# Mixture of 14 experts: GpSimd's indirect transfers in bursts of four, each burst gated by a pair of tiles

## The reference, cut to what matters

```python
x = x + 0.5 * L0_ffn(layernorm(x))          # attention and a mixture of 8
x = x + L0_attn(layernorm(x))               # linear attention
x = x + 0.5 * L0_ffn(layernorm(x))
x = x + 0.5 * L1_ffn(layernorm(x))          # mixture of 14, first call
x = x + L1_attn(layernorm(x))               # causal attention
return x + 0.5 * L1_ffn(layernorm(x))       # mixture of 14, second call

def L1_ffn(x):                              # x: 4096 tokens x 128
    probs = softmax(x @ gate_w.T)           # 14 experts
    top2_p, top2_i = top_k(probs, 2)
    w = top2_p / top2_p.sum(-1)
    all_out = gelu(x @ w1[e] + b1[e]) @ w2[e] + b2[e]     # hidden 256
    moe_out = w[0] * all_out[top2_i[0]] + w[1] * all_out[top2_i[1]]
    return clip(x + moe_out, -100, 100)
```

## Time and profile before

| | |
|---|---|
| time, median of 3 runs | 4130.89 us (4130.76 to 4134.79) |
| the profiled execution: span | 4133.9 us |
| TensorE busy | 3634.7 us (88%) |
| VectorE busy | 3108.4 us (75%) |
| ScalarE busy | 2040.9 us (49%) |
| GpSimd busy | 1267.6 us (31%) |
| granted TensorE clock, mean over the span | 0.943 |

### The profile page before, as it was taken

One profiled execution on the slowest core, in us unless ns is written; L12 is line 12 of the kernel. 1 busy time (PEld: TensorE's weight loads), 2 busy tenths in 40 slices (PEclk: granted clock), 3 DMA queues, 4 the chain that ended last, 5 costly groups with the idle time before them and its releaser, 6 DMA issues. The chain is left out here.

```text
span 4133.9 us, 60386 instructions
## 1 busy us (share of the span) xinstructions
PE 3634.7 (88%) x20845; PEld 1603.4 (39%) x20845; DVE 3108.4 (75%) x7157; ACT 2040.9 (49%) x3136; POOL 1267.6 (31%) x1378
## 2 busy tenths in 40 slices
PE   6999999989888779999998896647999999999865
PEld 2222222254445422222224445533444444444555
DVE  7999999467566699999993785456777777877444
ACT  2577777631343337777775123323444444444433
POOL 1011011011311201101101123434666676676543
PEclk8899999999999879999999997878999999999887
DMA  4211111220200041111115002322000000000133
GB/s 114 60 53 56 55 56 54 91 66 0 77 1 1 12 110 51 55 56 55 54 47 157 1 11 78 88 61 72 2 2 2 2 7 7 2 10 5 43 99 95
DMA packets 330712, 192.85 MB, mean 47 GB/s; under 512 B 172194, under 2 KB 285626, under 8 KB 330410
## 3 DMA queue, kind: packets, MB, share of 16 engines
q1 hardware_dynamic: 314634, 155.93, 14.1%
q0 software_dynamic: 14048, 32.79, 2.7%
q10 hardware_dynamic: 1728, 0.28, 0.0%
HBM read 119.74 MB, written 67.90 MB: 45 GB/s over the span
## 5 line engine op out<-in xcount | busy, mean ns | idle before, releaser
L877 DVE TENSOR_REDUCE ra_mh<-PS 128x1 f32<-128x512 f32 x2048 | 1309.2, 686 | 55.1 <-PE PS L737 34.7
L819 ACT ACTIVATE ra_p<-PS 128x1024 f32<-128x1024 f32 x1024 | 992.0, 1019 | 310.2 <-PE PS L745 309.8
L754 PE MATMUL PS<-ra_p,ra_va 128*32 128x512 f32 x4096 | 565.6, 606 | 0.3
L745 PE MATMUL PS<-ra_q,ra_k 75*128 75x512 bf16 x2048 | 538.5, 383 | 3.8 <-ACT ra_p L819 1.5
L2703 ACT ACTIVATE ca_p<-PS 128x1024 f32<-128x1024 f32 (+3 forms) x384 | 305.2, 811 | 369.6 <-PE PS L2596 366.2
L2774 POOL TENSOR_TENSOR ca_s<-ca_s,ca_p 128x1024 f32<-128x1024 f32 (+3 forms) x256 | 414.7, 1620 | 65.2 <-ACT ca_p L2703 44.5
L737 PE MATMUL PS<-ra_k,ra_q 48*128 48x512 bf16 x1024 | 408.2, 399 | 17.2 <-DMA ra_qo<-q_parts 16.6
L737 PE MATMUL PS<-ra_ko,ra_qo 48*128 48x512 bf16 x1024 | 409.0, 399 | 9.4 <-DVE ra_mh L877 9.4
L737 PEld LDWEIGHTS PS<-ra_k,ra_q 48*128 48x128 bf16 x1024 | 95.0, 93 | 659.3 <-DVE ra_mh L877 374.6
L2592 PE MATMUL PS<-ca_q,ca_k 64*128 64x512 f32 (+3 forms) x1536 | 318.8, 495 | 0.0
L2613 PE MATMUL PS<-ca_p,ca_v 128*64 128x512 f32 (+3 forms) x1536 | 290.3, 498 | 1.6 <-POOL ca_p L2763 1.6
(11 more groups left out here) (270 smaller groups left out, 5654.5 us busy)
## 6 DMA issues: line engine op xcount, KB each, us to landing
ra_k<-k_parts SPq DMA_DIRECT2D x128, 144.0 KB
ra_q<-q_parts SPq DMA_DIRECT2D x128, 144.0 KB
ao_ot<-o_heads SPq DMA_DIRECT2D x16, 1024.0 KB, 9.0
o_heads<-rp_rot POOLq DMA_DIRECT2D x122, 128.0 KB, 4.2
f_xg<-expert_tokens SPq DMA_DIRECT2D x56, 256.0 KB, 3.5
expert_outputs<-f_yb SPq DMA_DIRECT2D x56, 256.0 KB
expert_tokens<-X SPq DMA_DIRECT2D x28, 256.0 KB
q_parts<-rp_parts SPq DMA_DIRECT2D x48, 128.0 KB
```

Source lines behind the costliest of these rows:

```text
L745: mm = pe.matmul(PS[:, j, :], K[0:KROWS, ub, j, (step % KT) * P:(step % KT + 1) * P], Q[0:KROWS, ub, j, (step // KT) * BT:(step // KT + 1) ...
L754: mm = pe.matmul(PS[VW * j:VW * (j + 1), 4, :], VA[:, ub, step % KT, j, :], PR[:, s % 2, j, :], start=(s % KT == 0), stop=(s % KT == KT - ...
L819: act.activation(PR[:, s % 2, PH * pair:PH * (pair + 1), :], PS[:, PH * pair:PH * (pair + 1), :], ACT.Exp, scale=float(DH) ** -0.5).then_i ...
L877: dve.tensor_reduce(mh[:, pair, KT * odd + t, h:h + 1], PS[:, 5 + number % 3, :], AX.X, ALU.max).then_inc(s_bank[number % 3], 1)
```

## The change

GpSimd's 96 transfers of a call now come from a table `PLAN`, which gives each of them a pair. Before each transfer GpSimd waits until that many pairs are finished (`pool.wait_ge(s_ev, 2 * pair)`). The table walks through the transfers with a running pair number that grows by 1/1.6 for each transfer and never lies before the point where the data can be ready (`ready`); each four transfers share the pair of their first. The gates that come out, by bursts of four:

| | first call | second call |
|---|---|---|
| send 2 | 9, 11, 14, 16 | none, 2, 5, 7 |
| fetch 0, first part | 19, 21 | 16, 18, 21 |
| send 3 | 24, 26, 29, 31 | 23, 26, 28, 31 |
| fetch 0, rest | 34, 36 | 33 |
| fetch 1 | 39, 41, 44, 46 | 36, 38, 41, 43 |
| fetch 2 | 49, 51, 54, 56 | 46, 48, 51, 53 |
| fetch 3 | 60, 60, 60, 60 | 60, 60, 60, 60 |

The send of batch 3 no longer waits for all fetches of batch 0; it comes as soon as the table thinks its slots ready. The positions of the combines follow from the same table, 2.5 pairs (`LANDING`) behind the planned time of their second transfer: in the first call from tiles 44 to 63, 87 to 106 and 109 to 128 to tiles 44 to 81, 84 to 101 and 104 to 121; in the second call from 40 to 59, 83 to 102 and 105 to 124 to 38 to 75, 78 to 95 and 98 to 115.

```diff
-    ORDER = [("send", 2), ("fetch", 0), ("send", 3), ("fetch", 1), ("fetch", 2), ("fetch", 3)]
...
-    COMBINE, free = {}, 0.0
-    for what, b in ORDER:
...
-                    COMBINE[int(free + 2.7 * (j + 1)) + 4] = (b, j)
...
+    RATE, BURST, LANDING = 1.6, 4, 2.5
+
+    def ready(what, b):
+
+        if what == "send":
+            return BEGIN[b] + PART[-1] + 1 if b in BEGIN else 0
+        return MAXT // 2 * (b + 1) + 1
+
+    PLAN, COMBINE, at = [], {}, 0.0
+    todo = {}
+    for step in range(2 * KT * 6):
+        if step < 2 * KT:
+            what, b = "send", 2
+        elif todo.get(("send", 3), 0) < 2 * KT and (at >= ready("send", 3) or todo.get(("fetch", 0), 0) == 2 * KT):
+            what, b = "send", 3
+        else:
+            what, b = "fetch", min(b for b in range(BATCH) if todo.get(("fetch", b), 0) < 2 * KT)
+        i = todo.get((what, b), 0)
+        todo[what, b] = i + 1
+        at = max(at, ready(what, b))
+        PLAN.append((what, b, i, min(int(at if step % BURST == 0 else PLAN[-1][3]), PAIRS)))
+        if what == "fetch" and i % 2 and b < BATCH - 1:
+            COMBINE[int(2 * (at + LANDING))] = (b, i // 2)
+        at += 1 / RATE
...
-                for what, b in ORDER:
-                    for i in range(2 * KT):
...
+                for what, b, i, pair in PLAN:
...
+                    if pair:
+                        pool.wait_ge(s_ev, 2 * pair)
+                    if what == "send":
+                        front.send(pool, b, i)
+                    else:
+                        fetch(b, i // 2, i % 2)
```

More of the change, by code:

```diff
@@ L2062, in ffn1 @@
                   if BEGIN[b] + at >= 0)
-    COMBINE, free = {}, 0.0
-    for what, b in ORDER:
[L2067 to L2072, removed]
-                    COMBINE[int(free + 2.7 * (j + 1)) + 4] = (b, j)
-        free += 2.7 * KT
-    assert len(COMBINE) == (BATCH - 1) * KT
+    RATE, BURST, LANDING = 1.6, 4, 2.5
[19 more added lines that the diff above has]
+        at += 1 / RATE
+    assert len(COMBINE) == (BATCH - 1) * KT and len(set(PLAN)) == 2 * KT * 6
     LOADS = {3: (0,), 4: (1, 2), 5: (3, 4), 6: (5, 6, 7)}
@@ L2260, in fetch @@
                                             bass.IndirectOffsetOnAxis(slot[:, k, n:n + 1], 0)).then_inc(s_yk[b % 2][j], 16)
-                for what, b in ORDER:
-                    for i in range(2 * KT):
[L2265 to L2271, removed]
+                for what, b, i, pair in PLAN:
+                    if (what, b, i) == ("send", 2, 0 if 2 in BEGIN else 3):
+                        for m in (6, 7):
+                            front.rstd(pool, m)
+                    if pair:
[4 more added lines that the diff above has]
+                        fetch(b, i // 2, i % 2)
                 if next_norm:
```

## The result

The changed kernel takes 4063.9 us (median of 4 runs, 4051.4 to 4068.85), against 4131.96 us before (median of 4 runs). The ratio is 0.9824, with a 95% interval of 0.9805 to 0.9844. The profiled execution has a span of 4066.4 us, 67.5 us less than the 4133.9 of before. The forecast was 4060.

What follows compares the result with a forecast made beforehand. It took the bound to be a slow state the engines enter under GpSimd's continued indirect transfers in ffn1. Gains of 42 and 29 us, 71 in all, took 4133.9 to 4063, less 3.0 to 4060; range 3995 to 4118.

Steps and rivals of the forecast that it cites:

- The bound, and where the loss sits: In ffn1's two calls, tiles slow around GpSimd's five bursts of sixteen: late TensorE completions under continued indirect transfers, not bytes.
- The ceiling of 127 us: Most the change can give in ffn1: 70 us lost to bursts in the first call, 57 us in the second.
- 1.4 us a burst: Assumed loss for each burst of four in ffn1, from average idle before the first late tile; forecast range 0.7 to 2.
- The sum: Over both ffn1 calls, 42 us gained in the first and 29 us in the second, 71 us in all.
- Rival 1, joined bursts: In ffn1, two bursts act as one of eight, costing 2.75 us a burst: 17 us gained, 4114; chance 0.21.
- Rival 2, almost all comes back: In ffn1, four transfers always pass unseen and a burst loses 0.2 us or less: 119 us gained, 4012; chance 0.15.
- starved refill: Possible mechanism in ffn1's stalled stretches: instruction fetch starves under continued transfers, and a pause every 5 us lets refills through.
- Rival 3, no change: In ffn1, each transfer costs its 0.9 us wherever it stands, so spreading only moves the loss: 4131; chance 0.07.
- GpSimd as the bound: In ffn1, weight copies hold up each transfer, a pair takes 3.4 us, and 74 us eats the gain: 4131; chance 0.03.
- Rival 4, slower: In ffn1, every burst pays in full plus a restart of 1.7 us, 25 us a call: 4181; chance 0.09.
- The moved sending at nothing: Sending the fourth batch within the first's fetches in ffn1 costs nothing, with cover of some 4 pairs (over 8 us).
- Combines and the end: In ffn1, combines cost nothing with 2 us of cover, and the chain from the last sixteen fetches doesn't change.

Runs made afterwards that it cites:

- run with two powers after four: The kernel before, old order and no gates, with two small powers on GpSimd (about 1.1 us each) after every four indirect transfers: ratio 0.9762.
- row of 24: Unbroken row of 24 indirect transfers in the changed kernel with its gates removed, its order and combine places kept: ratio 1.0014.

## Why the prediction was right, and where two of its steps were not

The time came out 4 us from the forecast. Step by step:

- **The bound, and where the loss sits.** Right. It is the indirect transfers, in unbroken rows, through results of TensorE that arrive late. The ratio of 1.0014 without the gates, and loops of 143 and 135 us without the transfers, show it.
- **The ceiling of 127 us.** Too low: 147 us. The first call's part came near (70 worked out, 73.7 measured), the second's did not (57 against 73.0). Two errors are in it. The second call's sum priced 28 tiles with routing at 1.4 us, a price from the first call, from a stretch in which two batches are routed; in the second call one batch is routed, and the loop without transfers runs at 134.5 us for 120 tiles, 1.12 us a tile. And the sum took in the five stretches alone. Set pair by pair against the kernel without transfers, the stretches lost 67 us in the first call and 65 in the second, and 7 and 8.5 us more were lost between them. In the first call the price was too low instead (44 us of work, 48 without transfers), so the two errors had opposite signs there and that part is near by luck.
- **1.4 us a burst.** Too low: the loops still lose 36.6 and 45.7 us, 82 us in 40 bursts, 2.1 us a burst, just past the forecast's upper bound of 2. The step that failed is that a burst of four stays a burst of four. Set pair by pair against the kernel without transfers, the ten rows of eight lose 47 us, the row of thirteen 10 and the sixteen rows of four 25, which is 1.6 us a row and near the 1.4. With a pause of 2.5 us behind each, bursts of four cost 28.3 us over some 37 bursts in the two loops, 0.8 us, and that still holds the 8 us or so of the late fourth batch.
- **The sum.** 71 us forecast, 64 us in the loops. Two terms were short by 20 and 26 us, with opposite signs, so the sum was nearly right by luck, and not because each term was. By calls: 42 and 29 forecast, 37.0 and 27.3 measured.
- **Rival 1, joined bursts,** is what happened to a good part of the bursts, and its price came near: 2.75 us a burst, or 5.5 a row of eight. With bursts of eight the loops lose 57.7 and 56.9 us in ten bursts each, 5.7 us a row; here the ten rows of eight lose 4.7 each. In the first call seven of them hold 31 of the 36.6 us that are left. In the second, three hold 16 of the 45.7, the row of thirteen 10, and the ten rows of four 20: 2.0 a row, where the six of the first call lose 1.0. Why they cost more there isn't shown. I gave the rival the right mechanism (a gate 0.2 us wide) and too few consequences: by the mean of 2.5 pairs the pauses were to be 0.2 us, but gates that are 2 and 3 pairs apart in turn often make one pause of nothing and one of 4 us, as the table of gates showed already.
- **Rival 2, almost all comes back.** Not by this change. The run with two powers after four comes close: 147 - 28 = 119 us back in the loops. The starved refill that was put beside it falls: in the row of 24 no instruction packet was fetched between 2619 and 2643, and the engines went on at 2642.29 all the same.
- **Rival 3, no change.** Out: eight in a row cost 5.7 us and four with a pause 0.8, so the cost is not in proportion. GpSimd as the bound is out as well: its fetches take 0.985 us on average instead of 0.970. More of them overlap a weight copy, 49 of 128 instead of 26, and these take 1.04 us where the others take 0.95. So a copy does lengthen a transfer, which the average in the prediction hid, but by a tenth and not to the double.
- **Rival 4, slower.** Out. The granted clock rose from 0.943 to 0.951 over the span.
- **The moved sending at nothing.** Right under gates, within the error. It would have mattered otherwise: a pause without it made TensorE wait 5.99 us for those tokens.
- **Combines and the end.** About right: idle time before the combine's first line is 18.2 us instead of 14.8 in the whole kernel, and from the last tile to the end it takes 31.2 us instead of 30.9.

What stays open is which piece of hardware is held. The runs show that it is GpSimd's indirect form and not its bytes, that a break of 0.5 us with another instruction loosens it and one of 1.4 or 2.5 us nearly frees it (0.9 and 0.8 us lost a row of four), and that the signals of TensorE's results arrive late. Whether the result is late too, or only its signal, can't be read here. The Trainium skill, "Perfetto Trace Analysis" ("Tensor Engine Instruction (MATMUL, LD_WEIGHTS)"), says why a matmul's row doesn't tell: the end that the profiler gives a matmul is an estimate from its size, while the signal leaves only when the accumulator has taken all bytes. The row of 24 agrees, with a matmul that by its row ended at 2616.75 and a reader that began at 2642.29. A break needs no other instruction when it is long enough: bursts that a gate held apart for 1.5 us or more lost 1.6 us a row of four. Whether 0.5 us without one would do was not tried.

It also stays open what else a row must meet to stall TensorE. Just ahead of the first loop, in the kernel before, a row of sixteen runs beside the long matmuls of the mixture of 8 (in order of time):

```profile
2483.94 1.03 POOL L1972 DMA_INDIRECT expert_tokens<-XN,f_slot  x1 [0.17 <-issue]
...
2490.53 1.51 DVE L1268 SCALAR_TENSOR_TENSOR e_acc<-PS,e_w,e_acc 128x128 f32<-128x128 f32 x4 [1.29 <-PE PS L1146]
...
2494.65 3.60 PE L1146 MATMUL PS<-f_w,e_hT 128*128 128x512 f32 x8
...
2502.90 1.51 DVE L1268 SCALAR_TENSOR_TENSOR e_acc<-PS,e_w,e_acc 128x128 f32<-128x128 f32 x4 [4.72 <-remote]
```

From 2483.91 to 2498.69 TensorE works without a gap, and VectorE takes its results with waits of 1.3 us at most, though up to twelve transfers have gone. Only then, with TensorE at rest, does VectorE wait 4.72 us for a matmul that ended at 2498.25. So a long row alone doesn't stall TensorE everywhere; the costs found here are those of the mixture's short matmuls, with engines that wait for each other pair by pair.

## What to carry to other kernels

Look at a slow stretch by what another engine does at the time, not by the engine that waits: where the releaser in the trace had long been done, find whose burst ends just before the wait does. A gate by progress limits a burst only where the work between two gates is slower than the burst; look at the smallest distance between gates, not at the mean. And a pause that is always there can be worth more than one that asks whether it is needed, until it makes that engine late at the stage's end.

## What was not expected of the hardware

- In the pair loops, a row of indirect transfers holds back TensorE's results and costs about the time that it lasts beyond its fourth transfer: some 5 us in rows of eight, 13 to 17 in the rows of sixteen of the kernel before and 26 in the row of 24. Single results come through inside a row, and in the rows of eight and of 24 that are shown here the last wait ends 1.5 and 3.2 us after the row does.
- Direct transfers of the same 64 KB from the same queue, sixteen in a row, cost the loops nothing (142.6 us against 143.2 with none). Indirect ones with a quarter of the bytes cost as much as with all (222.3 against 216.9).
- The Trainium skill, "SBUF — State Buffer" ("SBUF: two separate sides"), holds that DMAs don't slow compute and that "PE, ACT, and DVE's dedicated pair never wait on anyone". What others see of TensorE was slowed here all the same: for 20 us beside nothing but indirect transfers, VectorE and ScalarE stood idle, with a matmul that they needed finished by its row. As the bytes don't matter and direct transfers cost nothing, the runs don't put this on a port of SBUF, and don't contradict the page there; they show that its rule doesn't cover GpSimd's indirect transfers.
